# Four stacked graph layers on one Trainium2 core: SP and ACT fetch one column of table rows in every second group

## The chip, the cores and the metric

The kernel runs on one NeuronCore of one Trainium2 chip. The metric is device time in microseconds (us) of one execution, lower is better. The engines named below are PE (TensorE), DVE (VectorE), ACT (ScalarE), POOL (GpSimd) and SP (SyncE, which only waits and issues transfers). Each engine runs its own list of instructions in order, and they meet at semaphores. A transfer (DMA) is issued by SP, ACT or POOL and carried out by 16 DMA engines that all three share.

## What is computed

Four graph layers follow one another on 12,500 nodes with 128 features and 200,000 edges sorted by their target node `dst`:

```python
h = relu(layernorm(x)); x = x + attention_1_head(h)            # layer a, batch norm behind it
h = relu(layernorm(x)); x = x + attention_4_heads(h, ea13)     # layer b, edge terms in the logit
h = relu(layernorm(x)); x = x + mlp([h, segment_sum(ea128, dst), u])
h = relu(layernorm(x)); x = x + relational(h)                  # layer rel, 8 edge types
# attention: logit = leaky_relu(a_src[src] + a_dst[dst] (+ a_edge)); softmax over the edges of one dst
#            out = segment_sum(softmax * h[src], dst)
# relational: out = relu(h @ W_self + segment_sum((h @ W_rel)[edge_type, src], dst) / degree)
```

What costs time is `h[src]`: for each of the 200,704 (padded) edges one row of a table in memory has to be fetched by its index. That happens three times: from `table_a` (130 floats a row), `table_b` (140 floats, 560 bytes) and `table_rel` (128 floats, 512 bytes; its row number is `src * 8 + edge_type`).

## The kernel before

Stages follow one another, with a semaphore between them: graph, sweep a, nodes a, sweep b, nodes b, sweep rel, nodes rel. The three sweeps go over all edges. The edges lie in 128 partitions of 1568 columns, and a sweep takes them in 98 groups (`NG`) of 16 columns (`GC`). For each group `g`:

- POOL issues 16 gathers (`indirect_dma_start`, L1111 in sweeps a and b, L2051 in sweep rel). One gather fetches 128 table rows, one to each partition, into a column of `rows[:, g % NS]`. There are `NS` = 6 such buffers in sweeps b and rel, 5 in sweep a. Before group g POOL waits until the store of group g - 6 has landed and group g - 5 and all before it are summed (`g - NS + 2` groups).
- DVE waits until the 16 gathers have landed, and then adds up the running sums of edges with the same target, in two steps of 8 columns. In sweep b it first forms the logits (L1257 to L1278), waits for ACT's exponentials (L1169), weights the rows (L1290), and joins (L1225, L1228). In sweep rel it multiplies the sums so far by `keep` (L2120) and adds (L2134), twice. The last operation counts up `summed`.
- ACT in sweep b computes the exponentials (L1169) and copies the edge terms into the rows (L1171); in sweep rel it copies `keep` to PSUM (L2081). In these two sweeps ACT also issues the store of the group before (L1125, L2072): `store(e, g - 1)` waits for `summed` and sends `rows[:, (g - 1) % NS]` (1120 KB or 1024 KB) to `sums_b` or `sums_rel`. In sweep a SP issues the stores, behind its loads of edge features.
- SP has nothing to do in sweeps b and rel but one load and the last transfers.

The order is written out by hand: it is the order of the Python loops. `natural(g, i)` gives the column of the index array for gather i of group g. `Gathers` keeps the counts that the waits need; the last group (97) has its first eight gathers on a semaphore of their own, since DVE takes it in two halves. The waits of DVE and POOL in sweep b:

```python
e.wait_ge(*stored[s].at(16 * (g // NS)))   # POOL, before group g: its buffer's last store has landed
e.wait_ge(*summed.at(g - NS + 2))          # and the buffer is no longer read
gathers.wait(e, g)                         # DVE, before group g: all 16 gathers have landed
```

## Time and profile before

| | us |
|---|---|
| median of 3 runs | 7913.9 (7896.88 to 7914.8) |
| the profiled execution, its own time | 7906.07 |
| its span, first to last instruction | 7894.7 |
| sweep a, first to last gather | 320.9 to 2504.4 |
| sweep b, first to last gather | 2933.0 to 5100.6 |
| sweep rel, first to last gather | 5562.9 to 7729.8 |

The times of the sweeps are the starts of their first and last gathers in the timeline. An engine's busy time is the time inside its instructions; what a group of instructions waited for stands behind it, with the releaser. "issue" means that the engine waited for nothing that the profile shows. POOL's gathers show a busy span of about 0.94 us and then some 0.30 us of "issue" before the next. An issue of a transfer by SP or ACT is shown as SPq or ACTq.

### The profile page before, as it was taken

The numbers are of one execution on the slowest core, as the hardware profiler recorded it, in microseconds if no ns is written. First come the engines' busy times: TensorE is split into PE (matmuls) and PEld (weight loads), VectorE is DVE, ScalarE is ACT, GpSimd is POOL, SyncE is SP. The second block draws the span as 40 slices with busy tenths as digits, with TensorE's granted clock in tenths as the row PEclk, the third lists the DMA queues.
The fourth block names the chain that finished last, engine by engine and source line by source line (L and its number), as shares of the span: only waits on it lengthen the run. The fifth ranks groups of instructions, "written<-read, shape, count | busy, mean of one in ns | idle before, by whom it ended". The sixth has DMA issues, their size and how long they took to land. (4 is left out here: it accounts for less than half of the span.)

```text
span 7894.7 us, 20407 instructions
## 1 busy us (share of the span) xinstructions
PE 647.8 (8%) x2458; PEld 431.7 (5%) x2458; DVE 3626.2 (46%) x6297; ACT 534.2 (7%) x1434; POOL 5330.8 (68%) x5327
## 2 busy tenths in 40 slices
PE   1100000000000430000000000069200000000000
PEld 1100000000000430000000000034100000000000
DVE  6656666676667565344433344367222222222223
ACT  1100000000000120000000000058000000000000
POOL 5676666666664567777777777621677777777776
PEclk7555555555555665555555555579555555555555
DMA  5456666665665423333333333345333222222322
GB/s 170 127 176 188 186 194 195 195 198 185 193 196 185 143 94 116 104 104 103 98 104 104 104 104 98 99 157 212 121 97 95 94 95 95 91 94 94 95 95 89
DMA packets 324460, 1042.91 MB, mean 132 GB/s; under 512 B 101449, under 2 KB 117964, under 8 KB 286434
## 3 DMA queue, kind: packets, MB, share of 16 engines
q0 software_dynamic: 175072, 371.37, 18.5%
q1 hardware_dynamic: 92914, 452.26, 16.7%
q10 hardware_dynamic: 56336, 217.99, 7.2%
q14 instruction: 119, 0.97, 0.0%
q8 instruction: 19, 0.31, 0.0%
HBM read 527.27 MB, written 513.96 MB: 132 GB/s over the span
## 5 line engine op out<-in xcount | busy, mean ns | idle before, releaser
L2051 POOL DMA_INDIRECT edge_rows<-table_rel,rel_row x1568 | 1602.6, 1022 | 673.5 <-issue 565.3
L1111 POOL DMA_INDIRECT edge_rows<-table_b,src_i x1568 | 1640.8, 1046 | 526.7 <-issue 525.9
L1111 POOL DMA_INDIRECT edge_rows<-table_a,src_i x1568 | 1480.0, 944 | 702.9 <-issue 479.8
L2134 DVE TENSOR_TENSOR edge_rows<-edge_rows,ps 128x1024 f32<-128x1024 f32 x195 | 238.0, 1221 | 1650.6 <-DMA edge_rows<-table_rel,rel_row 1647.3
L1257 DVE TENSOR_TENSOR z<-edge_rows,dst_logit 128x16 f32<-128x16 f32 (+2 forms) x198 | 40.3, 203 | 1174.0 <-DMA edge_rows<-table_b,src_i 1141.4
L1228 DVE TENSOR_TENSOR edge_rows<-edge_rows,ps 128x1032 f32<-128x1032 f32 (+1 forms) x390 | 484.2, 1241 | 190.1 <-remote 137.3
L1225 DVE TENSOR_TENSOR ps<-edge_rows,ps 128x1032 f32<-128x1032 f32 (+1 forms) x390 | 485.7, 1245 | 53.7 <-DVE edge_rows L1228 45.7
L1290 DVE TENSOR_TENSOR edge_rows<-edge_rows,ps 128x2064 f32<-128x2064 f32 (+2 forms) x198 | 456.5, 2306 | 92.5 <-issue 68.3
L1169 ACT ACTIVATE ps<-weight_decay 128x32 f32<-128x32 f32 (+2 forms) x198 | 47.6, 240 | 4099.4 <-issue 2264.2
L844 PE MATMUL ps<-ident,edge_rows 128*128 128x128 f32 x16 | 3.9, 426 | 3902.6 <-DVE edge_rows L1210 2227.9
L1210 DVE TENSOR_TENSOR edge_rows<-edge_rows,ps 128x1024 f32<-128x1024 f32 x195 | 237.0, 1215 | 91.4 <-remote 81.0
L1202 DVE TENSOR_TENSOR ps<-edge_rows,ps 128x1024 f32<-128x1024 f32 x195 | 239.0, 1226 | 58.2 <-DVE edge_rows L1273 58.2
L2120 DVE TENSOR_TENSOR ps<-edge_rows,ps 128x1024 f32<-128x1024 f32 x195 | 239.5, 1228 | 36.0 <-DMA edge_rows<-table_rel,rel_row 29.3
L1327 POOL DMA_INDIRECT node_sums<-sums_b,sum_row x98 | 95.5, 975 | 235.6 <-DVE out_b L1433 172.7
L844 PEld LDWEIGHTS ps<-ident,edge_rows 128*128 128x128 f32 x16 | 3.1, 224 | 3903.2 <-issue 2228.2
L1968 PE MATMUL ps<-w_rel,own_part 128*128 128x512 f32 x392 | 185.6, 611 | 10.5 <-DVE rel L1883 8.9
L949 PE MATMUL ps<-ident,edge_rows 128*1 128x128 f32 (+1 forms) x16 | 3.7, 413 | 2202.9 <-DVE edge_rows L1228 2202.9
L2081 ACT ACTIVATE ps<-keep 128x16 f32<-128x16 f32 x98 | 19.6, 201 | 2111.7 <-issue 1800.4
L1273 DVE TENSOR_TENSOR edge_rows<-weight_decay,z 128x8 f32<-128x8 f32 (+1 forms) x392 | 72.1, 184 | 187.7 <-remote 121.0
L1529 POOL DMA_INDIRECT dst_logit_b<-node_logit_b,start_row x98 | 99.0, 1011 | 86.5 <-DVE node_logit_b L393 57.8
L1327 POOL DMA_INDIRECT node_sums<-sums_a,sum_row x98 | 95.9, 978 | 79.5 <-issue 31.6
L524 POOL DMA_INDIRECT dst_logit_a<-node_logit_a,start_row x98 | 101.1, 1031 | 70.6 <-ACT node_logit_a L376 39.9
(284 smaller groups left out, 2933.1 us busy)
## 6 DMA issues: line engine op xcount, KB each, us to landing
sums_a<-edge_rows SPq DMA_DIRECT2D x98, 2064.0 KB
sums_b<-edge_rows ACTq DMA_DIRECT2D x98, 1120.0 KB
edge_rows<-in_ea SPq DMA_DIRECT2D x98, 1024.0 KB
sums_rel<-edge_rows ACTq DMA_DIRECT2D x98, 1024.0 KB
table_rel<-rel SPq DMA_DIRECT2D x98, 512.0 KB
edge_rows<-table_a,src_i POOLq DMA_INDIRECT x1568
edge_rows<-table_b,src_i POOLq DMA_INDIRECT x1568
edge_rows<-table_rel,rel_row POOLq DMA_INDIRECT x1568
```

The lines of the kernel that those rows point to most:

```text
L524: e.indirect_dma_start(out=A.dst_logit, out_offset=bass.IndirectOffsetOnAxis(ap=start_row[:, j:j + 1], axis=0), in_=node_a[:, j, :], in_of ...
L1111: e.indirect_dma_start(out=rows[:, s, i, 0:L.W], out_offset=None, in_=L.table, in_offset=bass.IndirectOffsetOnAxis(ap=src[:, at:at + 1], a ...
L1202: attr_step.append(then(e.tensor_tensor(old_attr, before(g, t)[:, :, L.W:L.WS], bc(keep_now[:, t, :].unsqueeze(2), [P, GK, D]), ALU.mult)))
L1210: done = e.tensor_tensor(now, now, old_attr, ALU.add)
L1225: done = then(e.tensor_tensor(heads(old), heads(before(g, t)), bc(decay_now.unsqueeze(3), [P, GK, H, C + 1]), ALU.mult))
L1228: done = e.tensor_tensor(now, now, old, ALU.add)
L1290: t_weight = then(e.tensor_tensor(now, now, bc(weights.unsqueeze(3), [P, (end - first) * GK, H, C + 1]), ALU.mult))
L1327: e.indirect_dma_start(out=self.buf[:, k % self.depth, b, :], out_offset=None, in_=self.sums, in_offset=bass.IndirectOffsetOnAxis(ap=sum_r ...
L1968: done = e.matmul(ps[:, 4 + 2 * (j % 2) + h, 0:half * D], own_part[:, j, :], w_rel[:, h * half:(h + 1) * half, :].rearrange("p r d -> p (r ...
L2051: e.indirect_dma_start(out=rows[:, s, i, :], out_offset=None, in_=table_rel, in_offset=bass.IndirectOffsetOnAxis(ap=rel_row[:, at:at + 1], ...
L2120: e.tensor_tensor(old, before, keep_now, ALU.mult).then_inc(step.sem, 1)
L2134: i = e.tensor_tensor(steps(g)[:, t, :, :], steps(g)[:, t, :, :], old, ALU.add)
```

## The change

In sweeps b and rel, every second group from 7 to 95 (45 groups, `helped_b = every(2, 7)`) loses its sixteenth gather on POOL. The 128 rows of that column are fetched one by one, each with a transfer of its own, by SP (partitions 0 to 63) and ACT (partitions 64 to 127). The row numbers are turned once, in the graph stage: the index columns of the helped groups (`helped_f`, 45 columns) are transposed by PE, so that the 128 numbers of one group lie in one partition of `helped_src` and `helped_rel`. SP and ACT load 32 of them at a time into 32 registers, and issue 32 transfers of one row. In each turn of its loop each of the two engines does one such batch of 32: a helped group needs two batches of SP and two of ACT, in four turns before it. All stores of sums in sweeps b and rel are now issued by SP, right when the group is summed. DVE waits in a helped group for two semaphores, the gathers' and the rows'. Sweep a is as it was.

```diff
+    def every(n, first):
+        return {g: h for h, g in enumerate(range(first, NG - 1, n))}
+    helped_b = every(2, 7)
...
+        def fetch(self, e, regs, g, p0, n):
+            if g not in self.place:
+                return
+            h, s = self.place[g], g % self.NS
+            e.wait_ge(*self.stored[s].at(16 * (g // self.NS)))
+            e.wait_ge(*self.summed.at(g - self.NS + 2))
+            for p in range(p0, p0 + n, len(regs)):
+                m = min(len(regs), p0 + n - p)
+                e.load(regs[0:m], self.index[h:h + 1, p:p + m])
+                for i in range(m):
+                    row = e.snap(regs[i])
+                    e.dma_start(self.rows[p + i:p + i + 1, s, LAST, 0:self.W], self.table[bass.ds(row, 1), :]
+                                ).then_inc(self.fetched[h % 3].sem, 16)
...
@@ graph stage, DVE and PE
+                then(e.memset(helped_f[:, :, :], 0.0))
+                e.tensor_copy(helped_f[:, 0, 0:len(helped_b)], helped_columns(tmp_e, helped_b)).then_inc(helped_floated.sem, 1)
...
+            e.wait_ge(*helped_turned.at(1))
+            then(e.tensor_copy(helped_src[:, :], ps[:, 7, 0:P]))
+            then(e.tensor_copy(helped_rel[:, :], ps[:, 7, P:2 * P]))
...
@@ sweeps b and rel, POOL
-                for i in range(GC):
+                for i in range(GC - (g in helped.place)):
...
@@ sweep b, SP, in each turn
+                e.dma_start(sum_rows(L.sums, g), rows[:, g % NS, :, :].rearrange("p (t k) w -> p t (k w)", t=GS)
+                            ).then_inc(stored[g % NS].sem, 16)
+                if L.AE:
+                    helped.fetch(e, regs_sync, g + 4, 0, P // 4)
+                    helped.fetch(e, regs_sync, g + 3, P // 4, P // 4)
...
@@ sweep b, ACT, in each turn
-                if attr is None and g >= 1:
-                    store(e, g - 1)
...
+                    helped.fetch(e, regs_scalar, g + 3, P // 2, P // 4)
+                    helped.fetch(e, regs_scalar, g + 2, 3 * P // 4, P // 4)
...
@@ sweep rel, ACT, in each turn
-                if g >= 1:
-                    store(e, g - 1)
-            store(e, NG - 1)
+                helped.fetch(e, regs_scalar, g + 2, P // 2, P // 4)
+                helped.fetch(e, regs_scalar, g + 1, 3 * P // 4, P // 4)
...
@@ DVE, before a group
-                        gathers.wait(e, g)
+                        e.wait_ge(*gathered[g % NS].at(helped.by_pool[g]))
+                        helped.wait(e, g)
```

POOL before, from the start of sweep b to the start of the transfers that end sweep rel (`first_logit` and `border_head` are small gathers; an x with a number is how often a row repeats):

```order
L1111 DMA edge_rows<-table_b,src_i 128x140 x9
L732 DMA first_logit<-node_logit_b,dst_first 128x4
L1111 DMA edge_rows<-table_b,src_i 128x140 x1559
L908 DMA edge_rows<-sums_b,head_row 128x140 x8
L1327 DMA node_sums<-sums_b,sum_row 128x140 x98
L2051 DMA edge_rows<-table_rel,rel_row 128x128 x1568
L2058 DMA border_head<-sums_rel,head_row 128x128 x8
```

POOL after, the same stretch (line numbers are shifted by the added lines):

```order
L1155 DMA edge_rows<-table_b,src_i 128x140 x9
L774 DMA first_logit<-node_logit_b,dst_first 128x4
L1155 DMA edge_rows<-table_b,src_i 128x140 x1514
L950 DMA edge_rows<-sums_b,head_row 128x140 x8
L1370 DMA node_sums<-sums_b,sum_row 128x140 x98
L2096 DMA edge_rows<-table_rel,rel_row 128x128 x1523
L2103 DMA border_head<-sums_rel,head_row 128x128 x8
```

The order is the same, and 45 gathers are gone from each of the two sweeps (1559 to 1514 behind the first 9, and 1568 to 1523).

ACT before, at the start of sweep rel, its first turns with the copy of `keep` and the store of the group before:

```order
L2076 DMA w_self<-in_d_self_wT 128x128
L2077 DMA b_self<-in_d_self_b 128x128
L2081 ACTIVATE ps<-keep 128x16 x2
L2072 DMA sums_rel<-edge_rows 128x2x1024
L2081 ACTIVATE ps<-keep 128x16
```

ACT after, at the same place, up to the first pair of its first batch (31 such pairs follow, and then the next turn's copy):

```order
L2122 DMA w_self<-in_d_self_wT 128x128
L2123 DMA b_self<-in_d_self_b 128x128
L2127 ACTIVATE ps<-keep 128x16 x6
L247 TENSOR_LOAD helped_rel
L249 ISA
L250 DMA edge_rows<-table_rel 1x128
```

A turn of ACT was one copy and one store. Now it is one copy, one load of 32 registers, and 32 pairs of a register operation (ISA) and a one-row transfer. The store is gone to SP.

SP after, in sweep b, from the end of one batch into the next; before, SP issued nothing here:

```order
L250 DMA edge_rows<-table_b 1x140
L1191 DMA sums_b<-edge_rows 128x2x1120
L247 TENSOR_LOAD helped_src
L249 ISA
L250 DMA edge_rows<-table_b 1x140
```

The store of a group has come in between two batches, so it is queued behind the rows of one and ahead of the rows of the other.

## Rows read from the trace of the kernel before

**Rows 1.** The page: busy time by engine; costly groups (busy us, mean ns | idle before, releaser)
```profile
PE 647.8 (8%) x2458; PEld 431.7 (5%) x2458; DVE 3626.2 (46%) x6297; ACT 534.2 (7%) x1434; POOL 5330.8 (68%) x5327
...
L2051 POOL DMA_INDIRECT edge_rows<-table_rel,rel_row x1568 | 1602.6, 1022 | 673.5 <-issue 565.3
L1111 POOL DMA_INDIRECT edge_rows<-table_b,src_i x1568 | 1640.8, 1046 | 526.7 <-issue 525.9
...
L2134 DVE TENSOR_TENSOR edge_rows<-edge_rows,ps 128x1024 f32<-128x1024 f32 x195 | 238.0, 1221 | 1650.6 <-DMA edge_rows<-table_rel,rel_row 1647.3
L1257 DVE TENSOR_TENSOR z<-edge_rows,dst_logit 128x16 f32<-128x16 f32 (+2 forms) x198 | 40.3, 203 | 1174.0 <-DMA edge_rows<-table_b,src_i 1141.4
```

**Rows 2.** Timeline of sweep rel, one turn (start us, duration us, engine, [idle before])
```profile
6435.01 1.22 DVE L2134 TENSOR_TENSOR edge_rows<-edge_rows,ps 128x1024 f32<-128x1024 f32 x1
6436.22 1.25 POOL L2051 DMA_INDIRECT edge_rows<-table_rel,rel_row  x1 [0.30 <-issue]
6436.27 0.37 ACTq L2072 DMA_DIRECT2D sums_rel<-edge_rows  x1
...
6438.34 1.94 POOL L2051 DMA_INDIRECT edge_rows<-table_rel,rel_row  x1 [0.87 <-issue]
6441.14 0.94 POOL L2051 DMA_INDIRECT edge_rows<-table_rel,rel_row  x1 [0.86 <-issue]
...
6452.38 0.95 POOL L2051 DMA_INDIRECT edge_rows<-table_rel,rel_row  x1 [0.30 <-issue]
...
6454.92 1.22 DVE L2134 TENSOR_TENSOR edge_rows<-edge_rows,ps 128x1024 f32<-128x1024 f32 x1 [17.42 <-DMA edge_rows<-table_rel,rel_row]
```

**Rows 3.** POOL by windows: from:to, length us, busy us (instructions), PEclk, DMA share, GB/s
```profile
800.00:1800.00 1000.00, 674.71 (x716) 0.50 0.62 193
...
2954.00:3154.00 200.00, 151.01 (x160) 0.50 0.39 115
3300.00:4300.00 1000.00, 758.62 (x716) 0.50 0.35 102
...
5563.00:5783.00 220.00, 166.37 (x177) 0.50 0.33 103
5900.00:6900.00 1000.00, 738.75 (x715) 0.50 0.30 94
```

**Rows 4.** Timeline, issues of transfers by SP and ACT at the start (start us, duration us)
```profile
1.19 0.45 ACTq L498 DMA_DIRECT2D src_i<-in_src  x1
...
1.66 0.45 ACTq L499 DMA_DIRECT2D typ_i<-in_edge_type  x1
...
25.36 0.22 SPq L484 DMA_DIRECT2D sums_b<-zero  x1
25.62 0.65 SPq L484 DMA_DIRECT2D sums_rel<-zero  x1
```

**Rows 5.** The same before nodes a: issues of SP one behind another
```profile
2590.71 0.43 SPq L1469 DMA_DIRECT2D bn_par<-in_a_bias  x1
2591.18 0.43 SPq L1469 DMA_DIRECT2D bn_par<-in_a_gamma  x1
```

**Rows 6.** Timeline of sweep b: what ACT does in one turn
```profile
4656.29 0.28 ACT L1169 ACTIVATE ps<-weight_decay 128x128 f32<-128x128 f32 x1 [21.79 <-issue]
4656.51 0.24 ACT L1171 ACTIVATE edge_rows<-edge_logit 128x64 f32<-128x64 f32 x1
...
4664.04 0.37 ACTq L1125 DMA_DIRECT2D sums_b<-edge_rows  x1
```

**Rows 7.** DMA queues, 2750 to 2920 us: scatters of 16-byte pieces (packets, MB, share)
```profile
q0 software_dynamic: 2784, 0.18, 1.9%
...
dst_logit_b<-node_logit_b,start_row POOLq DMA_INDIRECT x88
```

**Rows 8.** Timeline at the end of the graph stage
```profile
317.37 0.21 DVE L700 CAST sum_row<-s 128x98 int32<-128x98 f32 x1
317.67 1.48 ACT L737 ACTIVATE ps<-keep 128x1568 f32<-128x1568 f32 x1 [6.58 <-DVEq L171]
...
320.87 0.99 POOL L1111 DMA_INDIRECT edge_rows<-table_a,src_i  x1 [0.30 <-issue]
```

More of the change, by code:

```diff
@@ L707, in tensor @@
                     table.t_turn(e, i)
+            e.wait_ge(*helped_floated.at(2))
+            for i in range(2):
+                done = e.transpose(ps[:, 7, i * P:(i + 1) * P], helped_f[:, i, :], ident[:, :])
+            done.then_inc(helped_turned.sem, 1)
         return Programs(sync, scalar, gpsimd, vector, tensor)
@@ L1065, in attention_edges @@
         summed = sem_of("edges_summed", NG)
-        gathers = Gathers(NS)
+        helped = Helped(L.name, helped_b if L.AE else {}, helped_src, L.table, L.W, rows, NS, stored, summed)
+        gathered = [sem_of(f"edges_gathered{i}", helped.all_by_pool(i)) for i in range(NS)]
         def parts(g):
@@ L1108, in gpsimd @@
                     e.wait_ge(*summed.at(g - NS + 2))
-                for i in range(GC):
+                for i in range(GC - (g in helped.place)):
                     at = natural(g, i)
+                    landed = helped.first_half if g == NG - 1 and i < GK else gathered[s]
                     e.indirect_dma_start(
@@ L1113, in gpsimd @@
                         in_offset=bass.IndirectOffsetOnAxis(ap=src[:, at:at + 1], axis=0)
-                    ).then_inc(gathers.landed(g, i).sem, 16)
+                    ).then_inc(landed.sem, 16)
                     if g == 0 and i == GC // 2:
@@ L1119, in gpsimd @@
             crossing.p_head(e)
-        def store(e, g):
-            e.wait_ge(*summed.at(g + 1))
-            if L.AE:
-                e.wait_ge(*terms_copied.at(g + 1))
-            e.dma_start(sum_rows(L.sums, g), rows[:, g % NS, :, :].rearrange("p (t k) w -> p t (k w)", t=GS)
-                        ).then_inc(stored[g % NS].sem, 16)
         def sync(e):
@@ L2033, in edges_rel_stage @@
         summed = sem_of("edges_summed", NG)
-        gathers = Gathers(NS)
+        helped = Helped("rel", helped_b, helped_rel, table_rel, D, rows, NS, stored, summed)
+        gathered = [sem_of(f"edges_gathered{i}", helped.all_by_pool(i)) for i in range(NS)]
         crossing = Crossing("cross", rows[:, (NG - 1) % NS, GC - GK:GC, :], sb("border_state", [P, NV + 1])[:, :],
@@ L2048, in gpsimd @@
                     e.wait_ge(*summed.at(g - NS + 2))
-                for i in range(GC):
+                for i in range(GC - (g in helped.place)):
                     at = natural(g, i)
+                    landed = helped.first_half if g == NG - 1 and i < GK else gathered[s]
                     e.indirect_dma_start(
@@ L2053, in gpsimd @@
                         in_offset=bass.IndirectOffsetOnAxis(ap=rel_row[:, at:at + 1], axis=0)
-                    ).then_inc(gathers.landed(g, i).sem, 16)
+                    ).then_inc(landed.sem, 16)
             for g in range(NG - NS, NG):
@@ L2063, in sync @@
             crossing.q_load(e)
+            for g in range(NG):
+                e.wait_ge(*summed.at(g + 1))
+                e.dma_start(sum_rows(sums_rel, g), rows[:, g % NS, :, :].rearrange("p (t k) w -> p t (k w)", t=GS)
+                            ).then_inc(stored[g % NS].sem, 16)
+                helped.fetch(e, regs_sync, g + 4, 0, P // 4)
+                helped.fetch(e, regs_sync, g + 3, P // 4, P // 4)
             for g in range(NG - NS, NG):
@@ L2117, in vector @@
                         e.wait_ge(*keep_copied.at(1))
-                        gathers.wait(e, 0)
+                        e.wait_ge(*gathered[0].at(helped.by_pool[0]))
                     keep_now = bc(ps[:, 4 + g % 2, t * GK:(t + 1) * GK].unsqueeze(2), [P, GK, D])
@@ L2129, in vector @@
                     if t == 0 and g == NG - 1:
-                        gathers.wait_half(e)
+                        e.wait_ge(*helped.first_half.at(16 * GK))
                     elif t == 0 or g == NG - 1:
-                        gathers.wait(e, g)
+                        e.wait_ge(*gathered[s].at(helped.by_pool[g]))
+                        helped.wait(e, g)
                     e.wait_ge(*step.at(done))
@@ L2220, in _ @@
         def _(e):
+            regs_sync.extend(e.alloc_register(f"row_sync{i}") for i in range(32))
             graph.sync(e)
@@ L2238, in _ @@
         def _(e):
+            regs_scalar.extend(e.alloc_register(f"row_scalar{i}") for i in range(32))
             graph.scalar(e)
```

47 lines of the change are left out of this document (27 added, 20 removed).

## Prediction

> **What bounds the kernel now.** I read the page first. No engine fills the span: POOL is busiest with 68% and DVE has 46% [rows 1]. The waits tell more than the shares. In sweep rel DVE's first add of a group waits 1647.3 us in all for the gathers, and in sweep b its first logit operation waits 1141.4 us for them [rows 1]. POOL's own idle time in the same sweeps is "issue" (565.3 and 525.9 us): it waits for nobody, that is the step from one gather to the next. So in both sweeps POOL's row of gathers sets the end.
>
> The timeline of one turn of sweep rel shows the same closely. The last gather of the group starts at 6452.38, DVE starts on it at 6454.92, so a gather has landed 2.5 us after it started, and DVE had idled 17.42 us for it [rows 2]. DVE, ACT and the store are all done soon after, and the buffer that POOL wants next is six groups old.
>
> The pace of POOL is the number on which the sum rests. The windows give it [rows 3]. At the start of each sweep it is 160 gathers in 200 us and 177 in 220 us, 1.24 to 1.25 us each. Later it is 716 in 1000 us in sweep b and 715 in sweep rel: **1.398 us each**, 22.4 us for a group of 16. In the timeline the difference sits behind the store of sums: the gathers beside it take 1.25 and 1.94 us, with gaps of 0.87 and 0.86, where the others take 0.94 with 0.30 [rows 2]. But the mean is the same to a thousandth with stores and rows of different size (sweep rel and b), and even sweep a, with twice the transfer share (0.62 against 0.30), has 716 in 1000 us [rows 3]. That looks like a limit that counts gathers, not bytes or stores, with a reserve that is used up after the first stretch of each sweep.
>
> **What the change takes away.** Per sweep 45 gathers. At the steady pace this is 45 x 1.398 = 62.9 us, in two sweeps **125.8 us**. It is all on the path, since POOL waits for nobody and DVE waits for POOL. If only the gather's own time went (1.243, the pace without the later loss, 220/177), it would be 45 x 1.243 x 2 = 111.9 us. I take the first, by the equal pace of three unequal sweeps. What is late next: a mean turn is then 15.5 x 1.398 = 21.7 us. DVE was idle for 17.42 us of a turn in sweep rel, so it does not become the bound.
>
> **What it adds: the rows.** In 90 turns of each sweep SP and ACT each do one batch: a load of 32 registers, and 32 pairs of a register operation and a one-row transfer. None of the two stands in the trace of before, so I bound them.
> - The issue of a transfer. One row of 560 bytes without a register took 0.22 us, and the next issue started 0.26 us after it [rows 4]: the lower end. Transfers of 128 pieces follow each other on SP every 0.47 us [rows 5], on ACT every 0.47 us [rows 4]. The next one-row issue took 0.65 us, behind zero fills that were still draining [rows 4]; with a gap of 0.04 that is 0.69, the upper end. I take 0.40: one row is the nearer kind, but its address has to be worked out.
> - The register operation: between nothing and 0.2 us (the smallest operation of ACT here takes 0.24 [rows 6]). I take 0.05.
> - The load of 32 registers from SBUF: between 0.04 and the 2.5 us after which a gather has landed [rows 2]. I take 1.0.
>
> A batch is then 32 x 0.45 + 1.0 = 15.4 us, with 32 x 0.26 + 0.04 = 8.4 at the lower end and 32 x 0.69 + 2.5 = 24.6 or more at the upper. In sweep b ACT has besides its exponentials and copy, 0.28 + 0.24 [rows 6], and I allow 0.3 for semaphores: 16.2 us of 21.7. ACT idled for 21.79 us of its turn before [rows 6], so this is the cover. In sweep rel its own work is smaller. **I cost the rows at nothing**, as long as a batch with all this stays under 21.7 us, that is a pair under (21.7 - 1.8) / 32 = 0.62 us. The Trainium skill (DMA: Bandwidth & Descriptors, section "Latency and other measured facts") gives about 600 ns as the floor of a load into registers; with that a batch would be 0.4 us shorter, and no row here shows such a load.
>
> **Who waits behind the new waits.** `fetch` waits for the store of a group four or more groups back and for sums that were finished before; both are past when it comes. Behind ACT's batch is queued the exponential of the next group, on which DVE waits; behind SP's batch the store of the next group, on which POOL waits six groups later. Both come a whole turn later, so a batch of 16 us delays neither. The rows of a group are issued in the four turns ahead of it, and DVE finds them landed. The stores lose nothing on SP: ACT issued them at once too, 6436.27 right behind the add that began at 6435.01 and took 1.22 [rows 2].
>
> **Load on the shared DMA engines.** The nearest transfers with tiny pieces are the scatters behind nodes a: 88 of them made 2784 packets and took 1.9% of 16 engines in 170 us [rows 7], 51.7 / 88 = 0.59 us of engine time each. At that price 64 rows a turn take 37.6 of 16 x 21.7 = 347 us, 11%. The share rises from 0.30 or 0.35 [rows 3] to 0.41 or 0.46. That is no bound.
>
> **The graph stage.** One memset, two copies and two casts on DVE, two transposes on PE. DVE ends there at 317.58, ACT's first operation behind it starts at 317.67, and POOL goes on with its scatters and starts sweep a at 320.87 without a wait [rows 8]. A cast of this size takes 0.21 us, so some 1.5 us go into 3.3 us of cover: nothing.
>
> **Sum.** 7906.1 - 125.8 = 7780 against the profiled execution, which is 7.8 us below the median; against the median 7788. I predict 7784.
>
> **Rivals.**
> 1. *Only the gather's own time goes*, because the loss beside a store is paid per group: for it speaks that the slow gathers stand right behind the store's issue [rows 2], against it the equal pace of the sweeps. 7784 + 13.9 = 7798.
> 2. *The batches become the bound, slower than before.* If a pair takes 0.69 us, as the upper row has it, ACT's turn in sweep b is 32 x 0.69 + 1.8 = 23.9 us against 22.4 before. DVE then waits for the exponentials, and POOL for DVE once its six buffers are full. 90 turns x 1.5 us x 2 sweeps = +270: about 8180. It decides from 0.62 us a pair on, at 0.64 the gain is gone. The 0.47 of [rows 5] would leave 0.15 for the register operation, which is why this is my main doubt.
> 3. *No gain, since the rows come back to POOL by way of the shared engines.* The pace of 1.24 to 1.25 falls to 1.398 though the share is only 0.30 [rows 3], so something other than POOL does hold it back. If small transfers of SP and ACT count there, a rise by 3% to 1.443 cancels the gain (7910); one more step of 0.155, as from 1.243 to 1.398, makes a turn 15.5 x 1.553 = 24.1 us, 90 x 1.7 x 2 = +306, about 8215. A rule on this stands in the Trainium skill (DMA: Bandwidth & Descriptors, "Issuing engines are not separate DMA queues"): transfers begun on several engines run on the same 16 and save only the sequencer's time of issue. By that rule alone moving the rows saves nothing where the engines are the bound. Here it is just POOL's time of issue that sets the pace, by [rows 1] and [rows 3], so it speaks against the change only if the later pace is made by the engines.
> 4. *The change does not do what it says*: the rows land after the fifteen gathers, and DVE waits for them instead. At 15.4 us a batch and a turn of lead this needs a queue of SP or ACT that backs up; the end is again near 7910.
>
> **How the numbers follow.** Forecast 0.54, rival 1 0.12, rival 2 0.20, rival 3 0.07 without gain or loss and 0.05 slower, rival 4 0.02. A difference under 0.3% (24 us) can't be told from none. Faster are the first two: 0.66. Same: 0.09. Slower: 0.25. The range begins at 7765, if the pace eases a little where 15 gathers stand in a group. Up to no gain it holds 0.75; to hold 0.8 it takes in the mild end of rival 2, a pair of 0.655 us: 22.76 us a turn, 0.36 x 180 = +65, 7975.
>
> **What would show it.** Right: 1523 gathers of `table_b` and as many of `table_rel`; 715 gathers in 1000 us as before; each sweep 63 us shorter; DVE's wait of helped groups still ends with a gather of POOL; ACT and SP idle for 5 us or more of each turn. Wrong: a gap of ACT's exponentials that is filled by its own issues, DVE waiting for ACT, POOL waiting at the head of a group (rival 2); fewer than 700 gathers in 1000 us with ACT idle (rival 3); 15 x 1.25 with the whole loss behind the store (rival 1). The prediction falls first with the price of a pair, which I have from transfers without a register.

## The result: 22.5% slower, and the profile after

| | before | after |
|---|---|---|
| median of the runs, us | 7911.8 (7896.9 to 7914.8) | 9691.2 (9681.9 to 9699.0) |
| ratio | | 1.2251, 95% interval 1.2237 to 1.2266 |
| profiled execution, us | 7906.1 | 9686.8 |
| span, us | 7894.7 | 9681.0 |

The forecast was 7784, with a range up to 7975. Not the mild end of rival 2 came, but something far beyond it.

In most runs the kernel before took 7896 to 7947 us, but in those beside `e18`, `e20` and `e22` it took 7097 to 7101, on chips that had given 7907 and 7928 at other times, so each experiment is compared with the kernel before as it ran beside it.

The page of the changed kernel, its chain that ended last and its costliest groups (busy us, mean ns | idle us before, and what ended it):

```profile
SPq 35%; issue 30%; DVE 21%; another core or an unknown queue 5%; PE 3%; ACTq 2%; POOL 2%; ACT 1%; DMA 1%; POOLq 0%; DVEq 0%
...
L2096 POOL DMA_INDIRECT edge_rows<-table_rel,rel_row x1523 | 1436.8, 943 | 1652.9 <-DMA sums_rel<-edge_rows 1110.6
L1155 POOL DMA_INDIRECT edge_rows<-table_b,src_i x1523 | 1437.2, 944 | 1642.7 <-DMA sums_b<-edge_rows 1172.1
...
L2180 DVE TENSOR_TENSOR edge_rows<-edge_rows,ps 128x1024 f32<-128x1024 f32 x195 | 238.0, 1220 | 2290.7 <-DMA edge_rows<-table_rel 2210.3
L1333 DVE TENSOR_TENSOR edge_rows<-edge_rows,ps 128x2064 f32<-128x2064 f32 (+2 forms) x198 | 456.5, 2306 | 1045.3 <-ACT ps L1211 998.8
```

Set these against [rows 1]. The gathers are 45 fewer in each sweep, as written. POOL's busy time in them fell by more than they took, since a mean gather is now 943 or 944 ns long against 1022 and 1046. But POOL, which waited for nobody, now waits 2283 us for stores of sums, and DVE waits for the rows (`edge_rows<-table_rel`, not `table_rel,rel_row`), no longer for POOL. The chain runs through SP's queue. Windows of sweep b and sweep rel, with POOL's busy time and instructions, then clock, DMA share and GB/s:

```profile
3300.00:4300.00 1000.00, 0.00 (x0) 0.00 (x0) 263.81 (x398) 13.63 (x60) 449.41 (x477) 0.50 0.24 71
7600.00:8600.00 1000.00, 0.00 (x0) 0.00 (x0) 156.79 (x128) 6.43 (x32) 468.18 (x497) 0.50 0.21 68
```

477 and 497 gathers in 1000 us stand against 716 and 715 [rows 3]. The DMA engines carry less than before (71 and 68 GB/s against 102 and 94). One turn of sweep b (start us, duration us, engine, line; in brackets the idle time before):

```profile
4002.94 0.40 SPq L1191 DMA_DIRECT2D sums_b<-edge_rows  x1
...
4005.26 26.61 ACTq L250 DMA_DIRECT2D edge_rows<-table_b  x32
...
4007.44 0.94 POOL L1155 DMA_INDIRECT edge_rows<-table_b,src_i  x1 [13.86 <-DMA sums_b<-edge_rows]
4007.77 27.91 SPq L250 DMA_DIRECT2D edge_rows<-table_b  x32
...
4026.16 0.94 POOL L1155 DMA_INDIRECT edge_rows<-table_b,src_i  x1 [0.30 <-issue]
4035.79 0.40 SPq L1191 DMA_DIRECT2D sums_b<-edge_rows  x1
4036.74 0.22 DVE L1300 TENSOR_TENSOR z<-edge_rows,dst_logit 128x64 f32<-128x64 f32 x1 [26.88 <-DMA edge_rows<-table_b]
```

From one store to the next SP needs 32.85 us: the store, a load of 4.1, and 32 pairs in 27.9. That is a turn now, against 22.4 before. 180 turns of this length would lose 1880 us. Not all are that long: from first to last gather sweep b takes 3080 us against 2168 and sweep rel 2984 against 2167, together 1729 of the 1779 us lost. In the turn shown POOL does its 16 gathers at 1.25 us in 20 us and waits for the rest.

The pairs are not evenly slow. The chain of waits shows SP's longest records singly, ahead of and within the slow stretch (start us, us, what; L249 is the register operation, L250 a move and the transfer, "issue" a gap):

```profile
4009.30 0.05 issue
4009.35 0.07 SPq L249
4009.43 0.03 SPq L250
4009.46 0.03 issue
4009.49 0.23 SPq L250
4009.72 0.05 issue
```
```profile
4022.30 0.70 SPq L250
4023.02 0.69 issue
4023.70 0.70 SPq L250
4024.41 0.70 issue
```

At first a pair takes **0.42 us** (4009.30 to 4009.72). From 4010.6, 3 us after POOL's first gather, the recorded starts and ends of instructions come in steps of **0.70 us**, one or several of them at a step. 12 pairs go into the 19.4 us up to 4030.0, that is 1.6 us each. From then on, nearly 3 us after POOL's last gather ended, pairs take 0.42 again. I call this the hold. It is the subject of the experiments. A pair has three instructions. Where each start and each end has a step to itself, a pair takes six steps, 4.2 us; in this turn no pair does, but `e16` below has such pairs.

### The profile page after: what moved, and what is told of

The parts are those of the page before. It is cut to its first block, busy times and chain, and to the rows that moved or that the text cites. A ratio compares the mean times of both kernels' runs of the same rounds, so it can differ in the third digit from the quotient of the medians.

```text
span 9681.0 us, 55655 instructions
## 1 busy us (share of the span) xinstructions
PE 637.7 (7%) x2460; PEld 425.6 (4%) x2460; DVE 3619.7 (37%) x6302; ACT 534.1 (6%) x1434; POOL 4961.5 (51%) x5237
## 4 chain that ended last, share of the span: by engine, by line
SPq 35%; issue 30%; DVE 21%; another core or an unknown queue 5%; PE 3%; ACTq 2%; POOL 2%; ACT 1%; DMA 1%; POOLq 0%; DVEq 0%
SPq L250 20%; SPq L247 7%; SPq L249 7%; DVE edge_rows L1333 3%; DVE ps L1267 3%; DVE ps L1244 2%; DVE edge_rows L1252 2%; DVE edge_rows L1270 2%; ACTq L250 2%; POOL node_sums L1370 2%; DVE edge_rows L1316 1%; DVE edge_logit L1339 1%; DVE feat_prod L1327 1%; PE ps L2011 1%
## 5 line engine op out<-in xcount | busy, mean ns | idle before, releaser
L2096 POOL DMA_INDIRECT edge_rows<-table_rel,rel_row x1523 | 1436.8, 943 | 1652.9 <-DMA sums_rel<-edge_rows 1110.6
L1155 POOL DMA_INDIRECT edge_rows<-table_b,src_i x1523 | 1437.2, 944 | 1642.7 <-DMA sums_b<-edge_rows 1172.1
L1333 DVE TENSOR_TENSOR edge_rows<-edge_rows,ps 128x2064 f32<-128x2064 f32 (+2 forms) x198 | 456.5, 2306 | 1045.3 <-ACT ps L1211 998.8
```

Of the source, the lines that this page charges most:

```text
L1155: e.indirect_dma_start(out=rows[:, s, i, 0:L.W], out_offset=None, in_=L.table, in_offset=bass.IndirectOffsetOnAxis(ap=src[:, at:at + 1], a ...
L1333: t_weight = then(e.tensor_tensor(now, now, bc(weights.unsqueeze(3), [P, (end - first) * GK, H, C + 1]), ALU.mult))
L2096: e.indirect_dma_start(out=rows[:, s, i, :], out_offset=None, in_=table_rel, in_offset=bass.IndirectOffsetOnAxis(ap=rel_row[:, at:at + 1], ...
```

## Experiments

**Parts of the change.** First the change without its rows.

```diff
...
-                    e.dma_start(self.rows[p + i:p + i + 1, s, LAST, 0:self.W], self.table[bass.ds(row, 1), :]
-                                ).then_inc(self.fetched[h % 3].sem, 16)
```

> The change without the one-row transfers: SP and ACT load no registers and issue no rows, DVE does not wait for them; the column of 128 rows is left out in 45 groups of sweep b and 45 of sweep rel, so this is the change's gain without its cost. The 45 missing gathers per sweep and the stores on SP stay. Theory G (pace counts gathers, 1.398 us each): 7912 - 126 = 7786, and 715 gathers in 1000 us. Rival P (the loss beside a store is paid per group): 7912 - 112 = 7800, and fewer than 712 gathers in 1000 us, since 15 x 1.25 + 2.4 is 1.41 each in a helped group. A third, that the order of stores and waits is what made the change slow: over 9000.

7803.0 us beside 7928.1, ratio 0.9845 (0.9828 to 0.9861): 125 us gained, where the forecast had 125.8. The interval goes from 110 to 136 us, so the time alone does not tell this from the 112 of rival 1. The pace does, since it stayed:

```profile
3300.00:4300.00 1000.00, 0.00 (x0) 0.00 (x0) 404.29 (x598) 20.91 (x92) 754.60 (x715) 0.50 0.36 104
```

Next the kernel before with only the stores moved from ACT to SP.

> The kernel before with one part of the change alone: all stores of sums in sweeps b and rel issued by SP instead of ACT. Nothing is left out. Theory: the store starts at the same moment, 7912 within 8 us. Rival (the place of the store costs or gives something): over 7935 or under 7890.

7933.4 beside 7928.1, ratio 1.0004 (0.9994 to 1.0013): the stores' new engine costs nothing. Then the change with SP's half of the rows alone (ACT's two calls of `fetch` gone, the DVE wait halved).

> The change without ACT's half of the rows: ACT loads no registers and issues no rows (partitions 64 to 127 of the helped column are left out), SP issues its 32 a turn as in the change. Theory S (rows of SP and rows of ACT pass one and the same place, one after the other, beside POOL's gathers): SP's slow pairs fall from 1.40 to about 0.7 us, its batch from 27.9 to 18 to 20 us, and the time to 7800 to 8100. Rival O (the issue has its own price on each engine): SP's batch stays at 27 to 29 us, a turn at 32 to 33 us, and the time stays at 9600 to 9700.

9164.1, ratio 1.1552 (1.1531 to 1.1573), which neither theory had, but which is much nearer to theory O. SP's 32 pairs still take 24.4 us in a turn of 29.7, though half as many transfers are made:

```profile
4015.89 0.40 SPq L1191 DMA_DIRECT2D sums_b<-edge_rows  x1
4021.05 24.38 SPq L250 DMA_DIRECT2D edge_rows<-table_b  x32
4045.54 0.40 SPq L1191 DMA_DIRECT2D sums_b<-edge_rows  x1
```

So SP and ACT do not slow each other much; SP is held without ACT's rows too. Now half as many groups, with batches of 16 rows on SP and 21 or 22 on ACT.

```diff
-    helped_b = every(2, 7)
+    helped_b = every(4, 7)
```

> The whole computation; every fourth group helped instead of every second (23 groups a sweep), its 128 rows spread: SP 16 rows a turn in four turns, ACT 22, 21 and 21 rows in three. At 0.87 us a pair and 4.1 us a load SP's turn is 16 x 0.87 + 4.5 = 18.5 us, ACT's 22 x 0.83 + 3.2 = 21.5 us, both under 22.4. Theory (the batch only has to fit into a turn of POOL): 46 gathers x 1.398 = 64 us less, 7848. Rival (rows slow POOL's gathers too, fit or not): 7912 or more.

8795.5, ratio 1.1096 (1.1077 to 1.1114), nearly 950 us above the theory's 7848: a mean price of 0.87 us a pair does not carry over. The same 16 pairs take 26.0 us in one turn, which lies wholly beside gathers, and 11.6 in the next, which begins as POOL starts the last gather of its row:

```profile
3504.11 26.04 SPq L250 DMA_DIRECT2D edge_rows<-table_b  x16
...
3539.24 11.64 SPq L250 DMA_DIRECT2D edge_rows<-table_b  x16
```

**Is it the stores behind the batch?** SP's rows alone, as above, with ACT issuing the stores again.

```diff
-                e.dma_start(sum_rows(L.sums, g), rows[:, g % NS, :, :].rearrange("p (t k) w -> p t (k w)", t=GS)
-                            ).then_inc(stored[g % NS].sem, 16)
...
+                if L.AE and g >= 1:
+                    b_store(e, g - 1)
```

> The changed kernel with SP's half of the rows only and ACT issuing the stores of sums b and rel as before, so that no store is queued behind a batch of rows. The second half of each helped column is left out (it keeps old data). Theory B (the length of a batch sets the turn): SP's turn is the 29.6 us of the kernel with SP's rows alone less the store's 0.4, about 29.2, DVE waits for the rows and not for POOL: 9164 - 0.4 x 180 = 9090. Theory Q (the harm comes from the stores behind the batch, which hold up POOL, while the rows alone have a lead of three or four turns): POOL is free, the turn goes back towards 22 to 24 us, 7800 to 8200.

9314.2 beside 7907.0, ratio 1.178 (1.1746 to 1.1815), no better than 1.1552. POOL's wait moves from the store to DVE, DVE's wait for the rows stays, so the length of the batches is the cause, as theory B says, though it put the time 220 us too low. POOL's wait for the store, which fills the page of after, is a symptom.

**How many rows are free?** 4 and 16 rows in a batch in place of 32, in both sweeps and on both engines (one line of each is shown).

```diff
-                    helped.fetch(e, regs_sync, g + 4, 0, P // 4)
+                    helped.fetch(e, regs_sync, g + 4, 0, 4)
```

> The changed kernel with 4 rows in each batch of SP and of ACT instead of 32: 16 rows of a helped column come, the other 112 are left out. Theory E (each instruction of an engine is held to 1.40 us beside gathers, and a batch costs nothing as long as it fits into the turn): 4 pairs of 3 instructions are 16.8 us even if all are held, with a load and a store under 22.4 us: the time of the kernel without any rows, 7800 within 10 us. Theory L (each row costs its share of what 32 cost, (9691 - 7803) / 32 = 59 us): 7803 + 4 x 59 = 8040.

7797.3 beside 7905.6, ratio 0.9855 (0.9829 to 0.9882): the time without any rows. Four pairs beside gathers took SP 13.4 us in one turn, with their issues up to 4.2 us apart, and cost nothing, since the turn has 22.

> The same with 16 rows in each batch, 64 of a helped column's 128. Theory E: 16 x 3 instructions no longer fit beside gathers. Taken down from the turn of 32.85 us with 32 rows, 16 pairs fewer at the quiet 0.42 and a load shorter by 1.3 (2.8 instead of 4.1) leave 24.8 us; from the 29.5 us of the kernel with SP's rows alone they leave 21.5, which fits. So 7800 to 8360, below theory L, which gives 7803 + 16 x 59 = 8750.

8517.8, ratio 1.0767 (1.073 to 1.0804): above theory E's 8360, below 8750. Between 4 and 16 rows a batch stops being free, as theory E has it; for 16 my count from quiet pairs was 160 us too low.

**What is held?** Rows from fixed places: one instruction each, no load.

```diff
...
-                    row = e.snap(regs[i])
-                    e.dma_start(self.rows[p + i:p + i + 1, s, LAST, 0:self.W], self.table[bass.ds(row, 1), :]
...
+                e.dma_start(self.rows[p:p + 1, s, LAST, 0:self.W], self.table[16 * p:16 * p + 1, :]
```

> The changed kernel, where SP and ACT fetch as many rows of the same size, but from fixed rows of the table: no load into registers and no register operations, one instruction a row instead of three. What is left out is that the rows are the right ones. Both theories: no 4.1 us load. Theory E (three instructions at 1.40 us each make the 4.2 us of a pair beside gathers): rows are 1.40 us apart beside gathers and some 0.27 otherwise; in the 19.3 us of a turn that were slow SP issues 14 rows, the other 18 take 4.9, with the store a turn of 24.6 us against 22.4 before: +2.2 x 180 = +400, about 8310. Theory T (the one-row transfer itself is what is held, 4.2 us beside gathers): 4.6 rows in 19.3 us, the other 27.4 take 7.4, a turn of 27.1 us: +850, about 8760, and rows 4.2 us apart beside gathers. Theory R (the register operations alone are held): rows 0.27 us apart all the time, a batch of 8.6 us, no bound, 7790 as without the rows.

8299.1 beside 7910.2, ratio 1.0496 (1.0475 to 1.0517). Theory E had 8310. SP's records beside gathers, still 0.70 us apart, now two for a row:

```profile
3521.93 0.70 SPq L246
3522.64 0.70 issue
...
3524.04 0.70 SPq L246
3524.74 0.70 issue
```

And with no transfer at all: 32 activations of 128x1 in each group of sweep b on ACT, added to the kernel before.

```diff
+                    for k in range(32):
+                        e.activation(extra[:, at:at + 1], ident[:, 0:1], ACT.Copy)
```

> The kernel before with 32 activations of 128x1 added to every group of sweep b on ACT, which issues neither a row nor a load: ACT has no transfer but the store there. Nothing is left out. Theory E (every recorded instruction beside gathers is held to 1.40 us, whatever it does): 14 of them in the slow 19.3 us of a turn, 18 more at 0.22, with ACT's own work a turn of about 24.5 us against 22.4: +190 us, about 8100, and the trace has them 1.40 us apart beside gathers. Theories T and R (only transfers, or only register operations and loads, are held on an engine that isn't POOL): they follow each other in about 0.22 us, 7 us in all, inside ACT's idle time: 7912.

8064.9 beside 7910.2, ratio 1.020 (1.018 to 1.0221); theory E had 8100. Activations of 0.20 us, each 1.40 us behind the last:

```profile
3522.82 0.20 ACT L1176 ACTIVATE extra<-ident 128x1 f32<-128x1 f32 x1 [1.20 <-issue]
3524.22 0.20 ACT L1176 ACTIVATE extra<-ident 128x1 f32<-128x1 f32 x1 [1.20 <-issue]
3525.63 0.20 ACT L1176 ACTIVATE extra<-ident 128x1 f32<-128x1 f32 x1 [1.21 <-issue]
```

So an instruction need be neither a transfer nor a register operation to be held: plain activations of ACT pay up to 1.40 us as well. POOL is different. One memset in each of its groups:

```diff
+                e.memset(extra[:, NG + g:NG + g + 1], 0.0)
```

> The kernel before with one more instruction on POOL in each group of sweeps b and rel: a memset of 128x1, right ahead of the group's gathers. Nothing is left out. Theory E (beside gathers every recorded instruction of an engine is let through only at two steps of 0.70 us, which is why a gather takes 1.398 us and a row pair with its three instructions up to 4.2 us): the group becomes 17 x 1.398 instead of 16 x 1.398, +1.4 us in some 184 groups, +257 us, about 8170, and the windows show 673 gathers in 1000 us. Theory G (1.398 us is a matter of the gathers themselves, whatever else POOL does): the memset goes into POOL's own waiting, at most its own time of some 0.1 to 0.3 us a group, 7910 to 7960, and 715 gathers in 1000 us.

7917.6 beside 7910.2, ratio 1.001 (1.000 to 1.0019): theory G, not E. The 1.398 us is a matter of the gather. Of its rows or of the instruction? Each gather of sweep rel as two of 64 rows:

```diff
-                        out=rows[:, s, i, :], out_offset=None, in_=table_rel,
-                        in_offset=bass.IndirectOffsetOnAxis(ap=rel_row[:, at:at + 1], axis=0)
+                    for h in (slice(0, P // 2), slice(P // 2, P)):
...
+                            out=rows[h, s, i, :], out_offset=None, in_=table_rel,
+                            in_offset=bass.IndirectOffsetOnAxis(ap=rel_row[0:P // 2, at:at + 1], axis=0)
```

> The kernel before, where in sweep rel each gather of 128 rows is issued as two of 64 rows, and where ACT has 8 more activations of 128x1 in each group of that sweep, as a probe of the hold. As many rows of the same size are fetched; what is left out is that the second half of each column holds the rows of the first half. Theory N (what is worked off at 1.398 us is a gather's 128 rows, one after the other, and other engines' instructions stand in line behind them): the pace is 1.398 us for two gathers if POOL can issue one in 0.70 us, and the sweep keeps its 2190 us; if POOL needs more per gather, 1.25 us at most as for 128 rows, the sweep takes up to 32 x 1.25 x 98 = 3920 us (total up to 9640), and since 0.70 us of work then stands against 1.25 us of issue nothing is held: ACT's 8 follow each other within 0.3 us. Theory I (1.398 us is a price of each gather instruction, however many rows): 32 x 1.398 x 98 = 4384 us, total 10100, and ACT's 8 are 1.40 us apart.

10102.7 in a single run, where theory I had 10100. The window of sweep rel has 715 gathers of 64 rows in 1000 us, at half the DMA share, so the price is one of the instruction and not of its rows:

```profile
7000.00:8000.00 1000.00, 0.00 (x0) 0.00 (x0) 107.75 (x88) 21.48 (x198) 755.06 (x715) 0.50 0.16 47
```

**The load.** 8 registers a load instead of 32, on SP and in the same way on ACT.

```diff
-            regs_sync.extend(e.alloc_register(f"row_sync{i}") for i in range(32))
+            regs_sync.extend(e.alloc_register(f"row_sync{i}") for i in range(8))
```

> The changed kernel with 8 registers instead of 32: each batch of 32 rows loads four times 8 registers. Nothing is left out. If a load costs per register (4.1 us for 32 on SP, 2.8 for 16 in the kernel with every fourth group), the four take 4 x 1.0 = 4.1 us and the time stays at 9690 within 1%, beside gathers a little more for three more instructions of 1.4 us. If a load has a fixed price of some 1.5 us (4.1 for 32 against 2.8 for 16 leaves 1.5 for none), four loads take 4 x 1.5 + 32 x 0.08 = 8.6 us: +4.5 us a turn, +810 us, about 10500.

9580.2 beside 7907.0, ratio 1.2117 (1.2077 to 1.2157), 1.1% less than with 32. A load of 8 takes 0.79 us in the median, four of them 3.2: there is no fixed price of some 1.5 us. But the number of registers is not all. SP's 4.1 us for 32 stand right behind the store of sums. In `e15`, where SP issues no store, the same load took 2.07 us. The loads of `e14`, then of `e15`:

```profile
L247 SPq TENSOR_LOAD <-helped_src x360: 2/794/2561, 3058.2 to 5976.8; - x180
...
L247 SPq TENSOR_LOAD <-helped_src x90: 699/2068/2166, 3043.5 to 5825.4; - x90
```

(In such lines the three numbers are the shortest, median and longest time in ns.) Why a load behind the store takes twice as long was not tested.

**Does the hold last while gathers run, or only while they follow each other too fast?** The 32 activations again, and two memsets behind each gather of sweep b, so that gathers stand 1.91 us apart.

```diff
+                        for _ in range(2):
...
+                            e.memset(pad[:, :], 0.0).then_inc(padded.sem, 1)
```

> The kernel before with the 32 extra activations of 128x1 in each group of sweep b on ACT, and with two memsets of 128x320 on POOL behind each gather of that sweep, so that the gathers stand some 2 us apart instead of 1.25 to 1.40. Nothing is left out. The sweep takes 98 x 16 x some 2.0 us, about 1000 us more than before. Theory W (each gather brings 1.40 us of work that other engines' instructions stand behind; they are held only while that work is in arrears): gathers 2 us apart leave no arrears, and ACT's 32 follow each other in some 4 us as where POOL is idle. Theory P (while POOL is at gathers at all, another engine gets two steps per 1.40 us, or two per gather): ACT's 32 stand 1.40 us apart, or one gather's spacing apart, about 2 us, and then need more than the group's 32 us, so that ACT sets the end.

8169.8, but the kernel before took 7097.3 beside it, and sweeps a and rel of this run, which the edit doesn't touch, had gathers 1.248 us apart throughout. No hold was met, and the question stayed open. The same again:

> The kernel with spaced gathers in sweep b and 32 extra activations on ACT again. If the kernel before takes some 7910 in this call: theory W (arrears of work from gathers that follow each other faster than 1.40 us) expects ACT's 32 in some 3 us, as where nothing is held, and the sweeps a and rel at 1.398 us a gather: 8170 + 98 x 16 x 0.15 x 2 = 8640. Theory P (two steps per 1.40 us or per gather as long as gathers run) expects them 1.40 to 1.91 us apart, 45 to 61 us a group against 30.6: 9800 or more. If the kernel before takes some 7100, 8170 again.

8164.3 beside 7099.3: open again. And once more:

> The kernel with spaced gathers in sweep b and 32 extra activations on ACT once more, since both calls with it so far met the kernel before at 7100. If it takes some 7910 in this call: theory W (arrears of work from gathers that follow each other faster than 1.40 us; at 1.91 us apart there are none) expects ACT's 32 in some 3 us, and the sweeps a and rel at 1.398 us a gather: 8165 + 98 x 16 x 0.15 x 2 = 8635. Theory P (two steps per 1.40 us or per gather as long as gathers run, however far apart) expects ACT's 32 to stand 1.40 to 1.91 us apart, 45 to 61 us a group against 30.6, so that ACT sets the end: 9800 or more. If the kernel before takes some 7100, 8165 again, and the question stays open.

8768.2 beside 7927.6, theory W, though 133 us above its 8635 (P had 9800). In this one execution sweep b is free of the hold and sweep rel is not. Its windows of sweep b and rel, one group's activations, and a gather behind them:

```profile
4400.00:5400.00 1000.00, 0.00 (x0) 0.00 (x0) 287.20 (x427) 113.51 (x1122) 877.80 (x1552) 0.50 0.26 74
7300.00:8300.00 1000.00, 0.00 (x0) 0.00 (x0) 217.38 (x178) 8.85 (x44) 733.06 (x716) 0.50 0.30 93
```
```profile
4529.82 3.08 ACT L1185 ACTIVATE extra<-ident 128x1 f32<-128x1 f32 x32
...
4531.08 0.95 POOL L1115 DMA_INDIRECT edge_rows<-table_b,src_i  x1 [0.15 <-issue]
```

32 activations in 3.1 us beside running gathers. So the hold is there with gathers 1.25 us apart and not with gathers 1.91 us apart. Where between the two it begins was not measured; that it is at the 1.40 us to which it slows the gathers themselves is my inference.

**The change where no hold is met.** The changed kernel as it is, while the kernel before took 7099.3:

> The changed kernel as it is. In the call before this one the kernel before took 7097 us instead of 7907, and gathers stood 1.248 us apart for whole sweeps. If the kernel before takes some 7910 again, the changed one takes 9690 again. If it takes some 7100, theory H (the hold is what slows the changed kernel, and it is no part of the kernels' own work) expects pairs of 0.42 us throughout: a batch of 32 x 0.42 and a load of up to 4.1 is 17.5 us, in a turn of 15.5 x 1.248 = 19.3 us; with the store 17.9, so it fits narrowly, and the 45 gathers are gained: 7097 - 45 x 1.248 x 2 = 6985. Theory K (the batches are too long on any chip): a turn of 23 us or more, over 7400.

**6986.4 beside 7099.3, ratio 0.984 (0.9812 to 0.9869)**, where theory H had 6985. The same program is 1.6% faster here and 22.5% slower there. Its sweep b, and one turn of SP:

```profile
3300.00:4300.00 1000.00, 0.00 (x0) 0.00 (x0) 452.00 (x672) 23.63 (x104) 755.36 (x802) 0.50 0.41 120
```
```profile
4016.02 0.40 SPq L1191 DMA_DIRECT2D sums_b<-edge_rows  x1
...
4020.99 13.29 SPq L250 DMA_DIRECT2D edge_rows<-table_b  x32
...
4034.76 0.39 SPq L1191 DMA_DIRECT2D sums_b<-edge_rows  x1
```

Pairs of 0.42 us beside gathers 1.25 us apart: the batch, its load (4.3) and the store end 18.3 us after the last store began, in a turn of 15 x 1.248 = 18.7. It fits by 0.4 us. Then the two other kernels, to see whether their losses go as well:

> The kernel before with 32 activations of 128x1 in each group of sweep b on ACT, which took 8065 us where the kernel before took 7910. Nothing is left out. If the kernel before takes some 7100 in this call: theory H (the hold is a condition the run meets, and what it holds are instructions of every engine) expects ACT's 32 in some 3 us and no loss, 7100. If ACT's activations were slow for a reason of their own beside gathers, they stay 1.40 us apart and the loss stays near 150 us or more, 7250. If the kernel before takes some 7910 again, 8065.

> The kernel before with each gather of sweep rel issued as two of 64 rows and 8 activations more a group; the second half of each column holds the rows of the first half. It took 10103 us, 1.398 us an instruction, where the kernel before took 7907. If the kernel before takes some 7100 in this call, POOL's own step is left, which was 1.20 us for a gather of 64 rows in the stretches without a hold (8010 to 8021 us of that trace): 7100 + 98 x (32 x 1.20 - 16 x 1.248) = 8906. If 1.398 us were a price of each gather instruction on any chip: 7100 + 98 x (32 x 1.398 - 16 x 1.248) = 9527.

The kernel before took 7911.2 beside them, so they only repeat: 8068.1, ratio 1.0201 (1.0172 to 1.0231), and 10110.9, ratio 1.2784 (1.2747 to 1.2821), within 0.1% of the first times, on another chip.

## Why the prediction was wrong

**Right: what bounds the kernel, and what the gathers are worth.** 45 x 1.398 x 2 = 125.8 was measured as 125 without the rows, at an unchanged 715 gathers in 1000 us, so the first of the two readings of the pace held and rival 1 fell. "A limit that counts gathers, not bytes or stores" is what the split gathers showed. That the move of the stores is free was right too.

**Right: the price of a pair that nothing holds.** 0.40 + 0.05 was taken, 0.42 measured. Where no hold was met, the whole sum came out: 113 us gained, which is 45 x 1.248 x 2 = 112, the rows at nothing.

**Wrong: the step that took this price for one beside gathers.** The rows were costed at nothing as long as a pair stays under 0.62 us. In the mean of a batch a pair took 27.9 / 32 = 0.87, in the held stretch 1.6, so that a turn took 32.85 us in place of 21.7. Rival 2 named the mechanism, the deciding price and the signs in the profile: ACT's gap filled by its issues, DVE behind ACT (998.8 us), POOL waiting at the head of a group. They came, but larger waits stand beside them. DVE waits 3380 us in both sweeps for the rows themselves, the sign of rival 4, whose condition (a queue that backs up) was met, and POOL waits 2283 us for stores queued behind SP's batches, which the prediction had ruled out by its batch of 16 us. Rival 2's price of 0.69 came from rows near the kernel's start and at nodes a, where no gathers run. So did both bounds. That neither the load nor the pair stands in the trace of before was true, and I bounded what such an instruction costs by itself. The unknown that mattered was what any instruction costs in that stage. That the slow side was given 0.25 and rival 2 was the main doubt was sound; its size was not, +270 us against 1779.

**Wrong: the load.** 1.0 was taken, 4.1 measured on SP behind its store (bounds 0.04 and 2.5), 2.07 where SP issues no store. With quiet pairs that alone makes a turn of 18.3 instead of 15.8, which fits by 0.4 us. Alone it would have cost nothing, and the run without a hold shows it. The Trainium skill (DMA: Bandwidth & Descriptors, section "Latency and other measured facts") gives about 600 ns as the floor of such a load; 8 registers took 794 ns here, and 32 took seven times the floor. It is not quite a floor either: the 4 registers of ACT in `e16` took 0.49 us.

**Rival 3** said that rows of SP and ACT would slow POOL through the shared engines. They did not: POOL's gathers stand 1.25 us apart in the changed kernel, closer than before, and the DMA share fell to 0.24. The influence goes the other way. Gathers hold the instructions of SP and ACT, and they hold activations too, which move nothing over those engines. The rule of the Trainium skill (DMA: Bandwidth & Descriptors, "Issuing engines are not separate DMA queues") is neither shown nor refuted here; its resource was not the scarce one.

**What I could have read.** I saw that POOL's later pace was 1.398 in three unlike sweeps and explained it as POOL's alone. The trace of before shows the same number on another engine. DVE in sweep a, beside gathers:

```profile
1512.41 1.22 DVE L1210 TENSOR_TENSOR edge_rows<-edge_rows,ps 128x1024 f32<-128x1024 f32 x1 [1.84 <-remote]
1514.51 0.17 DVE L1273 TENSOR_TENSOR edge_rows<-weight_decay,z 128x8 f32<-128x8 f32 x1 [0.88 <-issue]
1515.91 1.23 DVE L1202 TENSOR_TENSOR ps<-edge_rows,ps 128x1024 f32<-128x1024 f32 x1 [1.23 <-DVE edge_rows L1273]
1517.31 0.17 DVE L1267 TENSOR_TENSOR weight_decay<-edge_rows,cut 128x8 f32<-128x8 f32 x1 [0.17 <-DVE ps L1202]
1519.41 0.17 DVE L1273 TENSOR_TENSOR edge_rows<-weight_decay,z 128x8 f32<-128x8 f32 x1 [1.93 <-remote]
1520.81 0.19 DVE L1277 TENSOR_TENSOR weight_decay<-z,edge_rows 128x16 f32<-128x16 f32 x1 [1.23 <-issue]
```

Whether an instruction takes 1.2 or 0.17 us, the next of these starts 1.40 or 2.10 us after it, in steps of 0.70. The idle time before it is put down to "issue", to "remote" or to a DVE operation that had ended up to 1.2 us before. Not every operation is held: two starts follow 1520.81 without a step. At 1.40 us for an instruction a turn of 22.4 us has room for 16 of them on an engine. The change puts 96 on SP and 96 on ACT. This sum needed no price of a pair, and it is warning enough. It does not give the size: at 1.40 us a batch would be 134 us, and SP's took 27.9, since POOL pauses and several records can share a step.

**What stays open.** What the hold is, and why some runs don't meet it. The same two chips did and didn't. The runs tell what it follows (gather instructions 1.25 us apart, not 1.91, and with 64 rows as with 128) and what it does (up to two steps of 0.70 us for an instruction of another engine, after some 3 us of full speed in the turn shown). They do not tell by what path. It isn't POOL's own count of instructions, since the memset was free.

**A rival that no run tests: the recording itself.** Each run here, the timed ones too, was recorded by the profiler, and the 0.70 us is also the pace of its records. The trace of the kernel before holds 1428 semaphore updates between 3300 and 4300 us, one in 0.70 us, though 715 gathers started there and each raises its semaphore by 16. Where no hold is met they are not missing: 20,779 updates in the same stretch of `e20`, and 125,823 in its whole trace against 40,138 in that of the run of 9687 us, for the same 55,655 instructions. `e25` has both in one execution, 9957 in 4400 to 5400 us (sweep b) and 1431 in 7300 to 8300 (sweep rel). The times of the held records are odd too. SP's issues of rows, first in the run of 9687 us, then in `e20` (shortest, median, longest in ns):

```profile
L250 SPq DMA_DIRECT2D edge_rows<-table_b x2880: 2/225/1399, 3048.0 to 6045.8; - x192
```
```profile
L250 SPq DMA_DIRECT2D edge_rows<-table_b x2880: 224/228/312, 2685.9 to 4421.5; - x192
```

An issue that needs 224 ns cannot be done in 2, so in the hold the recorded moments are not all those of the work. All this fits engines that wait until their records are taken, and it fits a third thing that slows both as well. If it is the recording, a run without it has no hold, and the change would gain there as in `e20`. The free memset speaks against a plain price for each record on POOL. The 22.5% stand for the runs as they were made, and "issue" or "remote" idle in a held stretch is a weak reading, because the update that would name the releaser may be missing.

## What to carry to other kernels

Price an operation that is added beside a stage from rows of that stage, and if there are none, look at how the small operations of any engine are spaced there: a common step in the starts, whatever the idle time is put down to, is a price per instruction that no quiet row shows. Then ask whether the step is the work's or the recording's: count the semaphore updates that the stage must make, and look for durations that are too short. Work that is moved from one instruction that does 128 rows to 384 small ones on two other engines is only as good as those engines' instruction rate in just that stage. And where the time depends on a condition that a run may or may not meet, here 1.6% gained against 22.5% lost, the change with the fewer instructions is the safer one.

## What the runs showed of the hardware that was not expected

- While gathers follow each other at POOL's own pace (1.25 us), an instruction of SP, ACT and, in the trace of before, DVE can take 1.40 us in these recorded runs, in two steps of 0.70; in long rows gathers themselves then average 1.398 us, with 128 rows or 64. In the same stretches most semaphore updates are missing from the trace (1428 of them beside 715 gathers that make 16 each).
- Gathers 1.91 us apart leave the other engines free: 32 activations in 3.1 us instead of up to 1.40 us each (`e25`).
- In some runs none of this is there: gathers at 1.248 us for whole sweeps, and the kernel before at 7099 instead of 7911 us, 10% less.
- A load of 32 registers from SBUF takes 4.1 us on SP right behind the issue of a large store and 2.07 without one (`e15`); 16 take 2.8 behind the store, 8 take 0.8 in the median. A one-row transfer with its register address takes 0.42 us of its engine when nothing holds it.
